# A two-layer recurrence on one core: x*Wx0 as 7 block products for 8, the second layer's recurrence in 256-column matmuls, the residual sums on GpSimd

## The chip, the cores and the metric

One of the eight NeuronCores of a Trainium2 chip runs the whole kernel. The time is the device time of one execution in microseconds (us). The kernel before took 2287.63 us (median of 3 runs, 2287.14 to 2290.14). The profiled execution took 2287.48 us; from its first to its last instruction, the span, it took 2285.6 us. TensorE's granted clock was 0.998 of full speed, its level of 2.4 GHz.

## The reference

`x` is 16 sequences of 512 steps of 512 values in float32. An LSTM of width 512 runs over it, its output is added to `x`, a tanh RNN of width 512 runs over the sum, and its output is added again.

```
# layer 0, for each step t
a = x[:, t] @ Wx0 + b0 + h @ Wh0                 # 16 x 2048
i, f, o = sigmoid(a[:, :1536]) in thirds;  g = tanh(a[:, 1536:])
c = f * c + i * g;   h = o * tanh(c);   y0[:, t] = x[:, t] + h
# layer 1, for each step s
k = tanh(k @ Wh1 + y0[:, s] @ Wx1 + b1);   y[:, s] = y0[:, s] + k
```

Both `h` and `k` start as `cond_1024`. No step of a layer can start before the state of the step ahead of it is there.

## The kernel before, in words

There are only 16 sequences, so TensorE gets the states as its stationary side (128 rows of the hidden dimension by 32 columns) and the weights stream past them. Four such matmuls run side by side, one for each 32 columns of the array (`tiles`, L175 to L180): they hold the same states, and each streams its own quarter (`q`) of the weights' columns into its own 32 partitions of a PSUM bank. "A group" below is such a set of four; a group with 256 columns covers 1024 outputs of one 128-row slice `k` of the contraction.

- **Input products, layer 0** (`input0`): two steps of `x` fill the 32 stationary columns. Four slices of 512 columns in float32 are the products of a pair of steps; one half of them is issued at every step. Each float32 matmul is issued as two instructions.
- **Recurrence, layer 0** (`recurrent0`): the state is split into a high and a low float16 part (2 x 16 columns), and so are the weights (`wh0_part`). A step has 2 halves of the outputs x 4 slices x 2 weight parts = 16 groups of 256 columns. The first half of the outputs holds all gates of the first half of the hidden units. ScalarE first writes the input products and the bias into the bank (`seed0`), the matmuls add to it.
- **Layer 1** runs `LAG` = 4 steps behind: `input1`, 2 groups of 128 columns in float32 a step, and `recurrent1`, 4 slices x 2 weight parts of 128 columns in float16.

TensorE's order in a step t is `recurrent0(t)`, a half of `input0` for a later pair, a half of `input1`, `recurrent1(t-4)`. While it does the last three, the cell of step t is worked out, one half of the hidden units after the other: VectorE turns the bank (`turn0`) and adds high and low part (`add0`); ScalarE does the gates (`gates`); VectorE the cell (`gate_products`, `cell`); ScalarE `tanh_cell`; VectorE the new state, rounded (`state_high`) and in full, and its low part (`state_low`), which sets `h0_ready[half]`. `recurrent0(t+1)` waits for `h0_ready[0]` ahead of slice 0 and for `h0_ready[1]` ahead of slice 2. Each engine follows its own written order (the `for t` loops at the end of each block), held to the others by semaphores alone.

The names in the profile are those of the tiles: `rec_ps` the banks of layer 0's recurrence, `in_ps` its input products, `rnn_ps` the bank that layer 1 uses for everything, `turned` what `turn0` (L353) or `turn1` (L403) wrote, `pre_sb` and `gate_ps` what `add0` (L359) wrote, `pre` what `add1` (L407) wrote, `uv` and `gates_cell` gates and cell. L365 is `gate_products`, L370 `cell`, L381 and L382 `state_high`, L389 `state_low`, L397 `add_y0`, L425 `add_y1`. All matmuls of the loop have the line L178.

## Time and profile before

| | |
|---|---|
| median of 3 runs | 2287.63 us |
| profiled execution, its span | 2287.48 us, 2285.6 us |
| TensorE matmul busy | 2242.9 us, 98% |
| VectorE busy | 1974.7 us, 86% |
| ScalarE busy | 1642.1 us, 72% |
| GpSimd busy | 1.8 us |
| TensorE's clock | 0.998 |

A busy share says how long an engine had something in it. Whether it sets the time is told by the chain of waits: who waited, for whom, and how long. "Idle before" in a group's row is the time that its engine stood still just ahead of it. Starts in a timeline are us from the start of the span.

### The profile page before, as it was taken

To read this page: it belongs to the slowest core of one execution; us is meant where nothing else is said; L and a number is where in the kernel's file an instruction comes from. 1 tells how busy PE (TensorE), PEld (TensorE's weight loads), DVE (VectorE), ACT (ScalarE), POOL (GpSimd) and SP (SyncE) were. 2 spreads that over 40 slices of the span, in tenths; PEclk is the share of its full clock that TensorE was granted. 3 is DMA by queue.
4 is the path that set the end of the run, shared out by engine and by line. 5 is a ranking of instruction groups with operands and counts; after the bars stand their busy time and mean duration, and the time that the engine had idled before them with its cause. 6 is when DMAs were issued, how large, how long until landed. Compare 5 with 4: busy or idle time off the path is not lost.

```text
span 2285.6 us, 150617 instructions
## 1 busy us (share of the span) xinstructions
PE 2242.9 (98%) x65564; PEld 1617.4 (71%) x65564; DVE 1974.7 (86%) x10283; ACT 1642.1 (72%) x5662; POOL 1.8 (0%) x10
## 2 busy tenths in 40 slices
PE   5999999999999999999999999999999999999997
PEld 2677777777777777777777777777777777777775
DVE  6888888888888888888888888888888888888887
ACT  5777777777777777777777777777777777777775
POOL 0000000000000000000000000000000000000000
PEclk9999999999999999999999999999999999999999
DMA  5000000000000000000000000000000000000000
GB/s 209 9 23 18 23 18 23 13 18 23 23 18 20 16 18 23 22 19 13 18 23 23 18 23 13 18 23 23 18 13 18 23 23 18 23 14 18 23 13 13
DMA packets 16738, 54.03 MB, mean 24 GB/s; under 512 B 2256, under 2 KB 2384, under 8 KB 14800
## 3 DMA queue, kind: packets, MB, share of 16 engines
q1 hardware_dynamic: 16080, 44.41, 5.5%
q8 instruction: 517, 8.47, 1.5%
q14 instruction: 141, 1.16, 0.2%
HBM read 27.62 MB, written 16.78 MB: 19 GB/s over the span
## 4 chain that ended last, share of the span: by engine, by line
PE 97%; DVE 2%; ACT 1%; issue 1%; POOL 0%; DVEq 0%; ACTq 0%; POOLq 0%
PE rec_ps L178 39%; PE in_ps L178 38%; PE rnn_ps L178 20%; ACT wh_part L478 1%; DVE largest_slice L277 0%; DVE turned L353 0%; DVE wh_part L321 0%; DVE uv L365 0%; DVE h_parts L381 0%; DVE pre_sb L359 0%; ACT gates_cell L502 0%; DVE h_parts L389 0%; ACT wx_sb L466 0%; DVE turned L403 0%; ACT rnn_ps L498 0%
## 5 line engine op out<-in xcount | busy, mean ns | idle before, releaser
L178 PE MATMUL in_ps<-wx_sb,x_sb 128*32 128x512 f32 x8192 | 977.4, 594 | 22.4 <-ACT wx_sb L466 22.4
L178 PE MATMUL rec_ps<-wh_part,h_parts 128*32 128x256 f16 x32704 | 988.9, 273 | 4.4 <-DVE h_parts L389 4.4
L178 PEld LDWEIGHTS rec_ps<-wh_part,h_parts 128*32 128x32 f16 x32704 | 867.5, 97 | 12.1 <-issue 7.0
L353 DVE STREAM_TRANSPOSE turned<-rec_ps 128x256 f32<-128x256 f32 x1024 | 460.4, 450 | 201.2 <-PE rec_ps L178 155.7
L178 PEld LDWEIGHTS in_ps<-wx_sb,x_sb 128*32 128x32 f32 x8192 | 258.9, 110 | 332.1 <-issue 318.9
L178 PEld LDWEIGHTS rnn_ps<-wx_sb,y 128*32 128x32 f32 x8192 | 247.0, 110 | 302.6 <-issue 301.1
L488 ACT ACTIVATE rec_ps<-in_ps,mask_scaled 128x256 f32<-128x256 f32 x1022 | 405.8, 434 | 2.0 <-PE in_ps L178 1.6
L178 PE MATMUL rnn_ps<-wh_part,h_parts 128*32 128x128 f16 x16352 | 323.4, 219 | 7.9 <-DVE h_parts L417 7.9
L178 PE MATMUL rnn_ps<-wx_sb,y 128*32 128x128 f32 x8192 | 318.4, 273 | 1.3 <-ACT rnn_ps L498 1.3
L502 ACT ACTIVATE gates_cell<-gate_ps,unscale 128x128 f32<-128x128 f32 x511 | 187.5, 367 | 181.2 <-DVE gate_ps L359 181.2
L498 ACT ACTIVATE rnn_ps<-rnn_ps,mask_scaled 128x128 f32<-128x128 f32 x511 | 174.8, 342 | 188.4 <-DVE turned L403 188.1
L178 PEld LDWEIGHTS rnn_ps<-wh_part,h_parts 128*32 128x32 f16 x16352 | 287.6, 97 | 9.2 <-ACT rnn_ps L498 5.5
L502 ACT ACTIVATE gates_cell<-pre_sb,unscale 128x128 f32<-128x128 f32 x511 | 205.3, 402 | 120.6 <-DVE pre_sb L359 120.5
L507 ACT ACTIVATE o_scaled<-gates_cell 128x32 f32<-128x32 f32 x1024 | 226.5, 221 | 16.1
L365 DVE SCALAR_TENSOR_TENSOR uv<-gates_cell 128x64 f32<-128x64 f32 x1024 | 227.2, 222 | 1.8 <-ACT gates_cell L502 1.3
L370 DVE SCALAR_TENSOR_TENSOR gates_cell<-uv 128x32 f32<-128x32 f32 x1024 | 196.8, 192 | 35.1
L389 DVE TENSOR_TENSOR h_parts<-h_full,h_parts 128x32 f16<-128x32 f32 x1024 | 192.0, 187 | 18.9
L512 ACT ACTIVATE tanh_c_sb<-gates_cell 128x32 f32<-128x32 f32 x512 | 117.6, 230 | 106.8 <-DVE gates_cell L370 106.7
L549 ACT ACTIVATE h_full<-pre,unscale 128x64 f32<-128x64 f32 x511 | 172.2, 337 | 2.3 <-DVE pre L407 2.3
L403 DVE STREAM_TRANSPOSE turned<-rnn_ps 128x128 f32<-128x128 f32 x512 | 162.0, 316 | 12.4 <-PE rnn_ps L178 3.2
L359 DVE TENSOR_TENSOR gate_ps<-turned 128x128 f32<-128x128 f32 x512 | 153.5, 300 | 17.6
L469 ACT ACTIVATE in_ps<-b_sb 128x512 f32<-128x512 f32 x256 | 150.9, 590 | 0.1
(52 smaller groups left out, 1272.9 us busy)
## 6 DMA issues: line engine op xcount, KB each, us to landing
x_sb<-xT SPq DMA_DIRECT2D x32, 512.0 KB, 3.7
yT<-y SPq DMA_DIRECT2D x64, 256.0 KB, 2.0
wh_sb<-wh SPq DMA_DIRECT2D x5, 1024.0 KB, 9.6
wx_sb<-wx SPq DMA_DIRECT2D x5, 1024.0 KB, 18.1
b_sb<-b SPq DMA_DIRECT2D x1, 256.0 KB, 2.7
b_sb<-b SPq DMA_DIRECT2D x1, 64.0 KB, 12.2
h_first<-h0T SPq DMA_DIRECT2D x1, 32.0 KB, 19.9
```

What stands on the lines that cost most here:

```text
L178: last = nc.tensor.matmul(out[QUAD * q:QUAD * (q + 1)], states, weights(q), start=False, stop=True, tile_position=(0, QUAD * q), skip_grou ...
L353: nc.vector.transpose(turned0[:, half].rearrange("p b n -> p (b n)"), rec0_ps[t % 2][half][:, 0:COLSH]).then_inc(turned0_done[half], 1)
L359: nc.vector.tensor_tensor(slices(pre0[half]), turned0[:, half, :, 0:BATCH], turned0[:, half, :, BATCH:], ALU.add).then_inc(pre0_done[half], 1)
L365: nc.vector.scalar_tensor_tensor(uv[:, half], gates_cell[:, half, 0:2], 1.0, gates_cell[:, half, 3:5], ALU.add, ALU.mult).then_inc(uv_done ...
L370: nc.vector.scalar_tensor_tensor(gates_cell[:, half, GATES], uv[:, half, 1], 0.5, uv[:, half, 0], ALU.mult, ALU.add).then_inc(cell_done[ha ...
L389: nc.vector.tensor_tensor(h0_parts[:, subs, BATCH:], slices(h0_full[:, cols]), h0_parts[:, subs, 0:BATCH], ALU.subtract).then_inc(h0_ready ...
L403: nc.vector.transpose(turned1[:, :].rearrange("p b n -> p (b n)"), rec1_ps).then_inc(turned1_done, 1)
L488: last = nc.scalar.activation(rec0_ps[t % 2][half][:, 0:COLSH], in0_ps[t // PAIR % 2][:, half * COLSH:(half + 1) * COLSH], ACT.Copy, scale ...
L498: nc.scalar.activation(rec1_ps, in1_ps[s // PAIR % 2], ACT.Copy, scale=own).then_inc(seed1_done, 1)
L502: nc.scalar.activation(gates_cell[:, half, 0:GATES].rearrange("p g n -> p (g n)"), pre0[half], ACT.Tanh, scale=unscale[0][:, :] if t else ...
L507: nc.scalar.activation(o_scaled[:, half], gates_cell[:, half, 2], ACT.Copy, bias=H_SCALE / 2, scale=H_SCALE / 2).then_inc(o_scaled_done[ha ...
L549: nc.scalar.activation(h1_full[:, :], pre1[:, :], ACT.Tanh, scale=unscale[1][:, :] if s > 1 else 1.0).then_inc(h1_full_done, 1)
```

## The change

**Seven products.** Four steps of `x` (a `SPAN`) are two pairs: the upper and the lower block row of a matrix X; the contraction has two halves, and so have the 512 columns. X*Wx0 is then a product of 2x2 blocks, done with 7 products and sums of blocks. Each is 2 slices of 256 columns: 14 units of one group, issued 4, 3, 4 and 3 to a step (`UNITS_OF_PART`), where the two pairs had 8 groups of 512 columns before. The sums of the blocks of `x` (`sum_x`, four for each 16 steps) and of the weights (`sum_wx0`, four at the start) are made by GpSimd. The sums on the side of the result are made where they accumulate (`z`, `v`, `c11`, `c12` in PSUM): ScalarE copies once or twice (`copy_v`, `begin_c11`), VectorE adds twice for each four steps (`begin_c12`, `finish_c22`). Two of the four `rec_ps` banks go to make room: the second half of layer 0 has one bank for all steps, and its seed is written in its own step.

**Layer 1.** High and low weights lie next to each other (`wh1_parts`): 4 groups of 256 columns for 8 of 128. Their sums are then four numbers for each output; one `tensor_reduce` adds them after a turn twice as wide. `seed1` writes half of the seed to each part.

**y.** `add_y0` and `add_y1` go to GpSimd, `add_y0` as two operations; VectorE's `h0_full` now waits for GpSimd to have read the one before (`h0_unscaled`). `input1` is split 3 slices and 1 for 2 and 2, so that each step has the same work. In `state_high` the full state becomes a step of its own, `state_full`, and the order of the second part of VectorE's step changes.

```diff
+SPAN = 2 * PAIR
+SPANS, PER_CHUNK = STEPS // SPAN, CHUNK // SPAN
+UNITS_OF_PART = (0, 4, 7, 11, 14)
+SLOTS = SPAN * SPANS - 5
...
+            def sum_wx0(i):
+
+                b11, b12 = wx0_sb[:, 0:SUBH, :, 0:COLSH], wx0_sb[:, 0:SUBH, :, COLSH:COLS]
+                b21, b22 = wx0_sb[:, SUBH:SUB, :, 0:COLSH], wx0_sb[:, SUBH:SUB, :, COLSH:COLS]
...
+                one, other = ((b12, b11), (b22, wx0_sums[:, 0]), (b22, b12), (b21, wx0_sums[:, 1]))[i]
+                nc.gpsimd.tensor_tensor(wx0_sums[:, i], one, other, ALU.subtract).then_inc(wx0_summed, 1)
...
+            for i in range(4):
+                sum_x(0, i)
+            reduce_largest(0)
+            for i in range(4):
+                sum_wx0(i)
...
+                nc.gpsimd.tensor_scalar(h0_true[:, :], h0_full[:, :], 1.0 / H_SCALE, None, ALU.mult).then_inc(h0_unscaled, 1)
+                pool.wait_ge(h0_unscaled, t + 1)
+                nc.gpsimd.tensor_tensor(y0[:, t // PAIR % Y0_PAIRS, :, t % PAIR], slices(h0_true[:, :]),
+                                        x_sb[:, v % 2, :, t % CHUNK], ALU.add).then_inc(y0_done, 1)
...
+            for t in range(END):
+                s = t - LAG
+                if 1 <= s:
+                    add_y1(s - 1)
+                if t < STEPS:
+                    add_y0(t)
+                if t == 1:
+                    reduce_largest(1)
+                v, c = divmod(t, CHUNK)
+                if 3 <= c < 7 and v + 1 < CHUNKS:
+                    sum_x(v + 1, c - 3)
...
+                products = (
+                    (z, lambda k: x_pair(g, 0, k), wx0_block(0, 0)),
+                    (v_ps[g % 2], lambda k: x_sum(g, 0, k), wx0_sum(0)),
+                    (z, lambda k: x_sum(g, 1, k), wx0_sum(1)),
+                    (c11_ps, lambda k: x_pair(g, 0, SUBH + k), wx0_block(1, 0)),
+                    (z, lambda k: x_sum(g, 2, k), wx0_sum(2)),
+                    (c12_ps, lambda k: x_sum(g, 3, k), wx0_block(1, 1)),
+                    (z, lambda k: x_pair(g, 1, SUBH + k), wx0_sum(3)),
+                )
...
-                        for part in weights:
-                            last = tiles(rec1_ps, states[:, k], lambda q: part[:, k, q])
+                    if s:
+                        last = tiles(rec1_ps, h1_parts[:, k], lambda q: wh1_parts[:, k, q].rearrange("p b w c -> p (b w c)"))
...
+                nc.vector.tensor_tensor(c12_ps, z_ps[g % 2], v_sb[:, :], ALU.add).then_inc(c12_begun, 1)
...
+                nc.vector.tensor_tensor(c22_sb[g % 2][:, :], z_ps[g % 2], v_sb[:, :], ALU.add).then_inc(c22_done, 1)
...
+            def state_full(half, n):
+
+                cols, subs = state_cols(half)
+                if n > 1:
+                    dve.wait_ge(h0_unscaled, n - 1)
                 nc.vector.tensor_tensor(h0_full[:, cols], o_scaled[:, half], tanh_c[half],
                                         ALU.mult).then_inc(h0_full_done[half], 1)
...
-                nc.vector.tensor_tensor(slices(pre1[:, :]), turned1[:, :, 0:BATCH], turned1[:, :, BATCH:],
-                                        ALU.add).then_inc(pre1_done, 1)
+                nc.vector.tensor_reduce(slices(pre1[:, :]), turned1[:, :, :, :].rearrange("p b r n -> p b n r"),
+                                        mybir.AxisListType.X, ALU.add).then_inc(pre1_done, 1)
...
+                    g, part = divmod(t + 5, SPAN)
+                    if t < SLOTS:
+                        if part == 2:
+                            begin_c12(g, t)
+                        elif part == 3:
+                            finish_c22(g, t)
                     turn0(0, t)
...
                     gate_products(1, n)
+                    state_high(0, n)
                     cell(1, n)
-                    state_high(0, n)
-                if rnn_state:
-                    add_y1(s - 1)
-                if lstm:
+                    state_full(0, n)
                     state_low(0, n)
                     state_high(1, n)
+                    state_full(1, n)
                     state_low(1, n)
                 if rnn:
                     turn1(s)
-                if lstm:
-                    add_y0(t)
-                if rnn:
                     add1(s)
...
+                if t < STEPS:
+                    act.wait_ge(slot_done, slots_until(t - 1))
...
+                    seed0(1, t)
+                    if ahead and part == 2:
+                        copy_v(g)
+                    if t + 1 < STEPS:
+                        seed0(0, t + 1)
```

Three places show how instructions move. The first is VectorE in the middle of the program, from the second half's gate products to the first turn of the next step. Before (L381 is `state_high` with the full state behind it in L382, L389 `state_low`, L425 and L397 the sums for y):

```order
L365 SCALAR_TENSOR_TENSOR uv<-gates_cell 128x64 [waits gates_done_1]
L370 SCALAR_TENSOR_TENSOR gates_cell<-uv 128x32 [waits uv_done_1]
L381 TENSOR_TENSOR h0_parts<-o_scaled,gate_ps 128x2x16 [waits tanh_c_done_0,o_scaled_done_0]
L382 TENSOR_TENSOR h0_full<-o_scaled,gate_ps 128x32
L425 TENSOR_TENSOR y1<-y0,h1_full 128x4x16
L389 TENSOR_TENSOR h0_parts<-h0_full,h0_parts 128x2x16 [waits h0_full_done_0]
L381 TENSOR_TENSOR h0_parts<-o_scaled,tanh_c_sb 128x2x16 [waits tanh_c_done_1,o_scaled_done_1]
L382 TENSOR_TENSOR h0_full<-o_scaled,tanh_c_sb 128x32
L389 TENSOR_TENSOR h0_parts<-h0_full,h0_parts 128x2x16 [waits h0_full_done_1]
L403 STREAM_TRANSPOSE turned1<-rnn_ps 128x128 [waits rec1_done]
L397 SCALAR_TENSOR_TENSOR y0<-h0_full,x_sb 128x4x16
L407 TENSOR_TENSOR pre1<-turned1 128x64 [waits turned1_done]
```

The same stretch of the changed program, where the next step is one with `begin_c12` (L519); L547 is `state_high`, L554 `state_full`, L561 `state_low`, L536 `cell`:

```order
L531 SCALAR_TENSOR_TENSOR uv<-gates_cell 128x64 [waits gates_done_1]
L547 TENSOR_TENSOR h0_parts<-o_scaled,gate_ps 128x2x16 [waits tanh_c_done_0,o_scaled_done_0]
L536 SCALAR_TENSOR_TENSOR gates_cell<-uv 128x32 [waits uv_done_1]
L554 TENSOR_TENSOR h0_full<-o_scaled,gate_ps 128x32 [waits h0_unscaled]
L561 TENSOR_TENSOR h0_parts<-h0_full,h0_parts 128x2x16 [waits h0_full_done_0]
L547 TENSOR_TENSOR h0_parts<-o_scaled,tanh_c_sb 128x2x16 [waits tanh_c_done_1,o_scaled_done_1]
L554 TENSOR_TENSOR h0_full<-o_scaled,tanh_c_sb 128x32 [waits h0_unscaled]
L561 TENSOR_TENSOR h0_parts<-h0_full,h0_parts 128x2x16 [waits h0_full_done_1]
L567 STREAM_TRANSPOSE turned1<-rnn_ps 128x256 [waits rec1_done]
L571 TENSOR_REDUCE pre1<-turned1 128x64 [waits turned1_done]
L519 TENSOR_TENSOR c1_ps<-in0_ps0,v_sb 128x256 [waits seed0_done_1,v_copied,slot_done]
L505 STREAM_TRANSPOSE turned0<-rec0_first_ps1 128x256 [waits rec0_done_0]
```

The first half's `state_high`, which waits for ScalarE's tanh, now stands ahead of the second half's `cell`; the two y sums are gone; two of four steps have a 256-column addition ahead of `turn0(0)`.

GpSimd at the start of the changed program (before, it had two ISA rows with the IOTA between them, and then the two reductions `largest_all`). An "ISA" row without names is a change of GpSimd's code library:

```order
L190 ISA
L190 IOTA partition 128x1
L223 TENSOR_TENSOR b0_diff<-b0_sb 128x256 [waits b0_doubled]
...
L209 TENSOR_TENSOR x_sums<-x_sb,x_sums 128x256 [waits x_summed]
L193 ISA
L193 ISA largest_all0<-largest0 128x1 [waits largest_done]
L220 ISA
L220 TENSOR_TENSOR wx0_sums<-wx0_sb 128x2048 [waits wx0_doubled]
...
L244 TENSOR_TENSOR y0<-h0_true,x_sb 128x4x16 [waits h0_unscaled]
L193 ISA
L193 ISA largest_all1<-largest1 128x1 [waits largest_done]
L242 ISA
```

There are now five changes of library for two, and three of them are behind the first sums.

## Rows read from the trace of the kernel before

**Rows 1.** The page: busy us, share of the span and instructions by engine.
```profile
PE 2242.9 (98%) x65564; PEld 1617.4 (71%) x65564; DVE 1974.7 (86%) x10283; ACT 1642.1 (72%) x5662; POOL 1.8 (0%) x10
```
**Rows 2.** Waits, whole span: us in total, times, longest.
```profile
PE rec_ps L178 <- DVE h_parts L389: 4.4, 6, 1.6
```
**Rows 3.** Timeline of TensorE, one step: start us, us, engine line op.
```profile
1201.05 1.93 PE L178 MATMUL rec_ps<-wh_part,h_parts 128*32 128x256 f16 x64
1202.79 1.90 PE L178 MATMUL in_ps<-wx_sb,x_sb 128*32 128x512 f32 x16
1204.51 0.62 PE L178 MATMUL rnn_ps<-wx_sb,y 128*32 128x128 f32 x16
1204.94 0.63 PE L178 MATMUL rnn_ps<-wh_part,h_parts 128*32 128x128 f16 x32
1205.39 1.93 PE L178 MATMUL rec_ps<-wh_part,h_parts 128*32 128x256 f16 x64
```
**Rows 4.** Timeline of the last steps, where TensorE has no input0.
```profile
2260.76 0.45 DVE L353 STREAM_TRANSPOSE turned<-rec_ps 128x256 f32<-128x256 f32 x1
...
2263.03 1.93 PE L178 MATMUL rec_ps<-wh_part,h_parts 128*32 128x256 f16 x64 [0.31 <-DVE h_parts L389]
2263.15 0.19 DVE L389 TENSOR_TENSOR h_parts<-h_full,h_parts 128x32 f16<-128x32 f32 x1
2263.26 0.31 DVE L403 STREAM_TRANSPOSE turned<-rnn_ps 128x128 f32<-128x128 f32 x1
...
2265.01 0.45 DVE L353 STREAM_TRANSPOSE turned<-rec_ps 128x256 f32<-128x256 f32 x1
```
**Rows 5.** Timeline of ScalarE, the same step as Rows 3.
```profile
1204.20 0.20 ACT L512 ACTIVATE gate_ps<-gates_cell 128x32 f32<-128x32 f32 x1
...
1204.75 0.23 ACT L512 ACTIVATE tanh_c_sb<-gates_cell 128x32 f32<-128x32 f32 x1 [0.21 <-DVE gates_cell L370]
```
**Rows 6.** Timeline of VectorE, the same step and the start of the next.
```profile
1203.03 0.45 DVE L353 STREAM_TRANSPOSE turned<-rec_ps 128x256 f32<-128x256 f32 x1
...
1204.53 0.19 DVE L370 SCALAR_TENSOR_TENSOR gates_cell<-uv 128x32 f32<-128x32 f32 x1
1204.64 0.18 DVE L381 TENSOR_TENSOR h_parts<-o_scaled,gate_ps 128x32 f16<-128x32 f32 x1
1204.73 0.18 DVE L382 TENSOR_TENSOR h_full<-o_scaled,gate_ps 128x32 f32<-128x32 f32 x1
...
1205.09 0.19 DVE L381 TENSOR_TENSOR h_parts<-o_scaled,tanh_c_sb 128x32 f16<-128x32 f32 x1
...
1205.41 0.19 DVE L389 TENSOR_TENSOR h_parts<-h_full,h_parts 128x32 f16<-128x32 f32 x1
...
1206.50 0.45 DVE L353 STREAM_TRANSPOSE turned<-rec_ps 128x256 f32<-128x256 f32 x1 [0.30 <-PE rec_ps L178]
1206.98 0.30 DVE L359 TENSOR_TENSOR gate_ps<-turned 128x128 f32<-128x128 f32 x1
```
**Rows 7.** Groups by form: busy us, mean ns of one, idle before.
```profile
L277 DVE TENSOR_REDUCE largest_slice<-wh_sb 128x1 f32<-128x512 f32 x4 | 2.5, 676 | 0.0
L488 ACT ACTIVATE rec_ps<-in_ps,mask_scaled 128x256 f32<-128x256 f32 x1022 | 405.8, 434 | 2.0 <-PE in_ps L178 1.6 <-issue 0.2
L407 DVE TENSOR_TENSOR pre<-turned 128x64 f32<-128x64 f32 x512 | 115.5, 226 | 0.1
L321 DVE SCALAR_TENSOR_TENSOR wh_part<-wh_sb,w_scale,wh_part 128x512 f16<-128x512 f32 x20 | 13.7, 746 | 1.5 <-ACT wh_part L478 1.5
```
**Rows 8.** Timeline of the start, GpSimd and VectorE.
```profile
12.33 0.13 POOL L167 IOTA partition<- 128x1 int32 x1 [10.85 <-issue]
...
22.27 0.38 POOL L170 PARTITION_ALL_REDUCE largest_all<-largest  x1 [9.81 <-DVE largest L277]
49.80 0.35 POOL L170 PARTITION_ALL_REDUCE largest_all<-largest  x1 [27.15 <-DVE largest L277]
...
58.53 0.18 DVE L382 TENSOR_TENSOR h_full<-o_scaled,gate_ps 128x32 f32<-128x32 f32 x1
```

More of the change, by code:

```diff
@@ L167, in _, with reduce_largest @@
             nc.gpsimd.iota(partition[:, :], [[0, 1]], 0, 1).then_inc(numbered, 1)
[L168 removed]
+            def reduce_largest(l):
                 pool.wait_ge(largest_done, l + 1)
@@ L243, in _ @@
                     recurrent0(0, h_first, [wh0_sb])
-                    for half in range(HALVES):
-                        input0(1, half)
+                    pe.wait_ge(seed0_done[0], 2)
+                    pe.wait_ge(c11_begun, 1)
+                    units(1, 2, UNITS_OF_PART[2])
                 elif t < STEPS:
```

262 lines of the change are left out of this document (186 added, 76 removed).

## The prediction, made before the changed kernel was run

> **What bounds the kernel now.** I read the busy shares first [rows 1]: TensorE has work in 98% of the span. The waits say that this is a true bound: TensorE waits for VectorE's new state (L389) for 4.4 us in the whole span, 6 times [rows 2], all in the first and last steps. The timeline of a step then gives its four parts [rows 3]: recurrence 1201.05 to 1202.79 (1.74), input products to 1204.51 (1.72), layer 1's input products to 1204.94 (0.43), its recurrence to 1205.39 (0.45). A step is 4.34 to 4.35 us, and 512 of them are 2225 of the span's 2285.6.
>
> The question is what comes next when TensorE gets less work, and the end of the trace answers it. There TensorE has no input products, so the recurrence alone sets the pace, and from one turn of the second half to the next it takes 2265.01 - 2260.76 = 4.25 us, with TensorE idle for 0.31 just ahead of it, released by L389 [rows 4]. So the loop through the state (turn, add, gates, cell, tanh, state, 16 groups) leaves only 0.10 us a step. Whatever TensorE saves beyond that is lost, and whatever the change puts into the loop counts in full.
>
> **What TensorE saves.** A float32 group of 512 columns takes 1.72 / 2 = 0.86, so one of 256 is taken at 0.43; layer 1's groups of 128 take 0.43 / 2 = 0.215, the same for each column [rows 3], so nothing is lost by short pieces. Units are 14 in four steps, 3.5 x 0.43 = 1.505 for 1.72. Layer 1's recurrence is 4 groups at 1.74 / 16 = 0.109, 0.436 for 0.45. With 1.74 and 0.43 as before a step of TensorE is 4.11, and 4 + 1 units are as long as 3 + 3 (1.935), so it is the same in each step. That is 0.23 less, 118 us in 512 steps, if TensorE stayed the bound. It does not.
>
> **The loop through the state.** It goes from the second half's turn to L389 (1205.41 - 1203.03 = 2.39 [rows 6]), and from there to the matmuls of slice 2 and the next turn. Three parts of the change touch it.
>
> 1. *The order in VectorE's queue.* The product for the second half starts 1205.09, and its tanh ended 1204.75 + 0.23 = 1204.98 [rows 5, 6]: 0.10 from the tanh's end to the product. The first half's tanh ends 1204.20 + 0.20 = 1204.40 [rows 5], so the first half's product can't start before 1204.50. Before, `cell` of the second half stood ahead of it and began 1204.53. Now `cell` stands behind that product, at the 0.10 that separates two small operations (1204.64, 1204.73 [rows 6]): 1204.60. That is +0.07 in the loop, in every step. Bounds: 0 (the tanh is seen sooner when nothing stands ahead of it) and +0.18, the product's whole duration. Taking y1's sum out of this stretch brings nothing, since the second half's product waited for the tanh and not for VectorE.
> 2. *The slack left in the 4.25.* L389 ends 2263.34 and slice 2's matmuls follow at 2263.03 + 4 x 0.109 = 2263.47 [rows 4], in their turn and not late, so some of those 0.13 may be slack. Bounds: 0, all of it is needed; and 0.10, since VectorE follows what it waits for by 0.03 (1206.50 + 0.45 to 1206.98 [rows 6]). I take 0.035, nearer to the end that is TensorE's own row. An ordinary step of the loop is then 4.25 - 0.035 + 0.07 = 4.285, over TensorE's 4.11 already; its bounds are 4.15 (both gains) and 4.43 (the product's 0.18, no slack).
> 3. *VectorE itself, in the two of four steps with a 256-column sum ahead of `turn0`.* The queue from L389 on: +0.11 to layer 1's turn (2263.15 to 2263.26 [rows 4]); that turn, 0.45 as the other turns of 256 columns, +0.03; the `tensor_reduce` R less the 0.08 by which the next starts ahead of its end; the sum C less 0.08; `turn0` to `add0` 0.48 (1206.50 to 1206.98); `add0` 0.22 [rows 6]; from the second turn to L389 again 2.39 + 0.07. In sum 3.59 + R + C. R: 512 elements take 0.676 [rows 7]; an element costs (0.45 - 0.31) / 128 = 0.0011 in the turns of 256 and 128 [rows 4, 6], so 256 take 0.676 - 0.27 = 0.41; below, 0.23, the addition it takes the place of (L407); above, 0.68, as if the strided reads cost twice. C: `add0` has 128 elements and takes 0.30 [rows 6], 512 take 0.75 (L321), so 256 take 0.44; bounds these two. The step is 3.59 + 0.41 + 0.44 = 4.44. In the other two steps the same queue, without the sum, is 4.44 - (0.44 - 0.08) = 4.08, under 4.285, and costs nothing.
>
> The mean is (4.285 + 4.44) / 2 = 4.36, 0.015 over the 4.345 of before: in the 504 steps in full swing +7.5 us. By R's bounds: 4.26 and 4.285 give 4.285 (-30 us), 0.68 gives 4.35 and 4.71, mean 4.53 (+93). By C's: 4.30 (mean 4.29, -27) and 4.75 (+87).
>
> **What costs nothing.** ScalarE gets 4 copies of 256 columns in four steps, 0.43 each [rows 7], for two of 512, and a `seed1` of 256 columns for 128: at most 0.43 + 0.14 a step on 1642.1 / 512 = 3.2 [rows 1], 3.8 of 4.36, all of it between its second tanh and the next step's gates. With that cover gone it would hold up the gates by what is over. The second half's seed, now in its own step, is asked for 0.87 later than the first's. On GpSimd y is three small operations a step. No row shows one; the nearest are VectorE's of 32 elements (0.18) and the partition reduction (0.38 [rows 8]), so 0.2 to 0.4 each, 0.9 for all; y0 is due about 3 us after the state. Above 1.4 each the queue would not keep up.
>
> **The port.** From rows nothing can be said on VectorE beside a busy GpSimd, which was busy 1.8 us in all [rows 1]. The Trainium skill, page "SBUF — State Buffer", section "Who interferes with whom", says that a VectorE instruction with two SBUF inputs and a GpSimd instruction that reads SBUF exclude each other, the first holding the port to its end. This speaks against the change, whose loop is full of such instructions; no run here shows it yet. The mechanism, in this kernel and priced from rows, is rival 2.
>
> **The start.** GpSimd now has five changes of code library. The first lies in the 10.85 ahead of the IOTA, beside the weights' DMAs; the second was over by 22.27 and can't be seen [rows 8]. So one costs 0 to 10.85; I take 7. The second now starts behind the sums of x, which I put at 19 by their place behind four weight tiles in SyncE's queue, and the first reduction is then at 26 for 22.27: +3.5. The first span's products come in another order, +1.5 to `seed0(0)`. The second reduction was at 49.80; now it is at 49.8 + 5 + 7 = 61.8, and behind it stands one more change, then y0 of step 2, whose reading VectorE's full state of step 3 waits for: 61.8 + 0.4 + 7 = 69 for 58.53 [rows 8], +10.5 in all; with 0 it would be +2, with 10.85 for each some +21. The Trainium skill, page "GPSIMD Engine Reference", section "2.1 Instruction dispatch", puts the first call to a freshly loaded library at about 6 us; by it the start would be about +7, and no run here shows it yet. The weights' sums, 4 x 2048 elements, end before they are due or hold it up by 1 or 2 us, which these bounds take in. The end, five steps of layer 1 alone, gets 0.13 + 0.19 a step for the wider turn and the reduction: +1.5.
>
> **The sum.** 2285.6 + 7.5 + 10.5 + 1.5 = 2305 of span; 2287.5 less 2285.6 lies around it, so 2307 of time. The profiled execution is within 0.2 us of the median.
>
> **Rivals.**
> 1. *TensorE stays the bound* (the loop is shorter than I read it): 2287.5 - 118 + 12 = 2182. For it: the waits of before. Against it: the 4.25 at the end, measured with less load on VectorE than now.
> 2. *GpSimd delays VectorE.* The full state releases at once L389, which is in the loop, and GpSimd's scaling for y0; y1's sum comes when `add0` does. If an operation of 0.2 to 0.3 is ahead of either, VectorE waits for its rest. At 0.13 a step it is 504 x 0.13 = +65 over mine, 2372; in every second step, 2340. For it: the loop has no slack to hide it. Against it: L389 follows the full state by 0.03, which leaves GpSimd little to be ahead by.
> 3. *On the other side of before: the loop has no detour through the first half's product.* The place is `cell` of the second half. If VectorE sees the first tanh 0.03 after its end, as it sees its own results, and not 0.10, `cell` starts where it did and both kinds of step lose 0.07: mean 4.29, -28, time 2287.5 - 28 + 12 = 2272. It decides from 0.05 on, where it eats the +20. R or C at half the way to their lower bounds gives the same or more. A shorter library change adds 5 to 8 in its favour.
> 4. *The start is worse*, each change of library as long as the first: +21, 2318. It lies inside the forecast's own range.
>
> **Chances.** Mine (2288 to 2325) 0.45, GpSimd in the way (2325 to 2375) 0.2, R or C larger with the same outcome 0.07, rival 3 (2250 to 2283) 0.2, rival 1 0.08. A measurement here tells apart 0.2%, 4.6 us. Slower 0.67, the same 0.07 (the low end of mine and the top of rival 3), faster 0.26. The range that leaves 2 in 10 out: 2252 to 2365.
>
> **What will show it.** TensorE's `rec_ps` group should have an idle time of 0.15 to 0.35 a step, over 80 us in all, released by `state_low` (L561), where it had 4.4. Steps should be of two lengths, near 4.28 and 4.44, in pairs. In VectorE's timeline `cell` of the second half (L536) starts 0.10 behind L547, and L547 0.10 behind the tanh's end. TENSOR_REDUCE of L571 has a mean of 410 ns, L519 and L526 some 440. The y operations on GpSimd show 200 to 400 ns. The second reduction is late by 10 us or so at 60. I am wrong if TensorE's idle time stays small (rival 1), if the steps are near 4.29 (rival 3), or if L561 and `add0` show longer durations or gaps while GpSimd is busy (rival 2).

## The result and the profile after

| | before | after |
|---|---|---|
| time, median | 2288.89 us (2287.14 to 2290.31) | 2352.13 us (2351.15 to 2353.26) |
| profiled execution: span | 2285.6 us | 2350.2 us |
| second half's turn of step 8 | 80.1 us | 105.2 us |
| mean step from 8 to 500 | 4.353 us | 4.427 us |

The ratio is 1.0277, with a 95% interval of 1.0259 to 1.0295. The direction was forecast and the time lies in the range, but I forecast +19 us and it was +63. The turns of the second half divide the 64.6 us of span: 25.2 up to step 8, (4.427 - 4.353) x 492 = 36.7 in the loop, 2.7 behind step 500.

The changed kernel's page, busy time by engine and its first groups, which answer to [rows 1]:

```profile
PE 2250.4 (96%) x63548; PEld 1741.2 (74%) x63548; DVE 2194.5 (93%) x9514; ACT 1782.6 (76%) x5919; POOL 648.0 (28%) x1679
...
DVE 77%; PE 12%; issue 10%; DMA 0%; ACT 0%; POOL 0%; SPq 0%; POOLq 0%; DVEq 0%; ACTq 0%
...
L273 PE MATMUL rec_first_ps<-wh_part,h_parts 128*32 128x256 f16 x16352 | 562.9, 275 | 52.9 <-DVE h_parts L561 27.2
```

VectorE has 86% turned into 93%, and the chain that ended last runs through it for 77% of the time; before, TensorE had 97% of it. So the bound has changed engine. TensorE's busy share of 96% hides that, since the ends of its matmuls are modelled. Its wait stands at the weight loads, on average 0.31 us in each of 491 steps, where I forecast 0.15 to 0.35. No releaser is shown for it; of the idle time of the matmuls themselves, 52.9 us, the row above puts 27.2 down to `state_low` (L561). The rows of the waits, after and before, which answer to [rows 2]:

```profile
PEld rec_first_ps L273 <- issue: 153.8, 491, 12.5
```
```profile
PEld rec_ps L178 <- issue: 11.6, 18, 3.0
```

The place of that wait differs from the one in the forecast. From step 100 to 480 the first matmul of `recurrent0`, which waits for the first half's state, starts 0.28 behind the one ahead of it (a matmul that waits for nothing follows by about 0.09); the first one of slice 2, which waits for the second half's state, starts 0.13 behind.

Two steps in four are long, as forecast. VectorE's timeline over one of them, which answers to [rows 6]:

```profile
1204.53 0.19 DVE L547 TENSOR_TENSOR h_parts<-o_scaled,gate_ps 128x32 f16<-128x32 f32 x1
1204.63 0.19 DVE L536 SCALAR_TENSOR_TENSOR gates_cell<-uv 128x32 f32<-128x32 f32 x1
...
1205.62 0.44 DVE L567 STREAM_TRANSPOSE turned<-rnn_ps 128x256 f32<-128x256 f32 x1
1206.10 0.59 DVE L571 TENSOR_REDUCE pre<-turned 128x64 f32<-128x256 f32 x1
1206.62 0.42 DVE L519 TENSOR_TENSOR c_ps<-in_ps,v_sb 128x256 f32<-128x256 f32 x1
1206.95 0.43 DVE L505 STREAM_TRANSPOSE turned<-rec_first_ps 128x256 f32<-128x256 f32 x1
1207.41 0.30 DVE L511 TENSOR_TENSOR gate_ps<-turned 128x128 f32<-128x128 f32 x1
```

From L567 to L511 VectorE never stands still for more than 0.04: its own queue is what lasts. `cell` (L536) stands 0.10 behind L547, as forecast. The groups by form, which answer to [rows 7]:

```profile
L571 DVE TENSOR_REDUCE pre<-turned 128x64 f32<-128x256 f32 x512 | 305.9, 597 | 17.4
L519 DVE TENSOR_TENSOR c_ps<-in_ps,v_sb 128x256 f32<-128x256 f32 x127 | 53.6, 422 | 0.0
L472 DVE SCALAR_TENSOR_TENSOR wh_part<-wh_sb,w_scale,wh_part 128x512 f16<-128x512 f32 x16 | 27.9, 1811 | 1.3 <-ACT wh_part L648 1.3
```

R is 597 ns where I put 410. L472, the low parts of `wh0` in the start, had a mean of 746 before [rows 7], here of 1811. The mean hides two sizes, as the view of that line shows (ns: least, median, most):

```profile
L472 DVE SCALAR_TENSOR_TENSOR wh_part<-wh_sb,w_scale,wh_part x16: 740/746/5042, 30.2 to 57.8; 128x512 f16<-128x512 f32 x16
```

Twelve of the 16 take 740 to 751; the other four take 4977 to 5042, one beside each of GpSimd's four sums of weights. The start on GpSimd and VectorE, which answers to [rows 8], first GpSimd, then VectorE:

```profile
28.10 0.38 POOL L193 PARTITION_ALL_REDUCE largest_all<-largest  x1 [10.25 <-issue]
35.96 4.56 POOL L220 TENSOR_TENSOR wx_sums<-wx_sb 128x2048 f32<-128x2048 f32 x1 [7.49 <-ACT wx_sb L624]
...
50.52 4.82 POOL L220 TENSOR_TENSOR wx_sums<-wx_sb,wx_sums 128x2048 f32<-128x2048 f32 x1
...
74.61 0.38 POOL L193 PARTITION_ALL_REDUCE largest_all<-largest  x1 [6.16 <-issue]
82.11 0.41 POOL L242 TENSOR_SCALAR h_true<-h_full 128x64 f32<-128x64 f32 x1 [7.13 <-issue]
```
```profile
33.11 2.74 DVE L472 SCALAR_TENSOR_TENSOR wh_part<-wh_sb,w_scale,wh_part 128x512 f16<-128x512 f32 x4 [0.15 <-ACT wh_part L648]
36.09 22.46 DVE L472 SCALAR_TENSOR_TENSOR wh_part<-wh_sb,w_scale,wh_part 128x512 f16<-128x512 f32 x8 [0.23 <-ACT wh_part L648]
```

Three library changes show (10.25, 6.16 and 7.13). And four low parts took 2.74 up to the moment at which GpSimd's sums of weights begin (35.96); the next eight took 22.46, to 58.55, of which the first four take 5.0 each, and the last four, behind the end of those sums at 55.34, 0.74 each.

### The profile page after: what moved, and what is told of

It is laid out like the page before. It is cut to its first block, busy times and chain, and to the rows that moved or that the text cites. A ratio compares the mean times of both kernels' runs of the same rounds, so it can differ in the third digit from the quotient of the medians.

```text
span 2350.2 us, 149629 instructions
## 1 busy us (share of the span) xinstructions
PE 2250.4 (96%) x63548; PEld 1741.2 (74%) x63548; DVE 2194.5 (93%) x9514; ACT 1782.6 (76%) x5919; POOL 648.0 (28%) x1679
## 4 chain that ended last, share of the span: by engine, by line
DVE 77%; PE 12%; issue 10%; DMA 0%; ACT 0%; POOL 0%; SPq 0%; POOLq 0%; DVEq 0%; ACTq 0%
DVE turned L505 14%; DVE h_parts L547 7%; DVE h_parts L561 7%; DVE turned L567 7%; DVE pre L571 6%; DVE uv L531 6%; DVE gate_ps L511 6%; DVE gates_cell L536 6%; DVE pre_sb L511 5%; DVE h_full L554 4%; PE rec_first_ps L273 3%; PE in_ps L273 3%; DVE h_parts L581 3%; PE rec_second_ps L273 3%; PE rnn_ps L273 2%
## 5 line engine op out<-in xcount | busy, mean ns | idle before, releaser
L273 PE MATMUL rec_first_ps<-wh_part,h_parts 128*32 128x256 f16 x16352 | 562.9, 275 | 52.9 <-DVE h_parts L561 27.2
L273 PE MATMUL rec_second_ps<-wh_part,h_parts 128*32 128x256 f16 x16352 | 537.7, 273 | 0.0
L273 PEld LDWEIGHTS rec_first_ps<-wh_part,h_parts 128*32 128x32 f16 x16352 | 362.0, 95 | 229.2 <-issue 152.4
L273 PEld LDWEIGHTS rec_second_ps<-wh_part,h_parts 128*32 128x32 f16 x16352 | 439.9, 97 | 9.0
L273 PE MATMUL in_ps<-wx_sums,x_sums 128*32 128x256 f32 x6096 | 400.7, 380 | 0.0
L273 PE MATMUL rnn_ps<-wh_parts,h_parts 128*32 128x256 f16 x8176 | 323.8, 273 | 10.4 <-DVE h_parts L581 10.4
L571 DVE TENSOR_REDUCE pre<-turned 128x64 f32<-128x256 f32 x512 | 305.9, 597 | 17.4
L670 ACT ACTIVATE rnn_ps<-rnn_ps,mask_scaled 128x256 f32<-128x256 f32 x511 | 228.2, 447 | 32.4 <-DVE turned L567 14.2
L273 PEld LDWEIGHTS rnn_ps<-wh_parts,h_parts 128*32 128x32 f16 x8176 | 230.7, 97 | 14.7 <-issue 7.3
L567 DVE STREAM_TRANSPOSE turned<-rnn_ps 128x256 f32<-128x256 f32 x512 | 226.7, 443 | 4.0 <-PE rnn_ps L273 4.0
L561 DVE TENSOR_TENSOR h_parts<-h_full,h_parts 128x32 f16<-128x32 f32 x1024 | 196.7, 192 | 36.0
L505 DVE STREAM_TRANSPOSE turned<-rec_second_ps 128x256 f32<-128x256 f32 x512 | 228.5, 446 | 0.3
```

What stands on the lines that cost most here:

```text
L273: last = nc.tensor.matmul(out[QUAD * q:QUAD * (q + 1)], states, weights(q), start=False, stop=True, tile_position=(0, QUAD * q), skip_grou ...
L505: nc.vector.transpose(turned0[:, half].rearrange("p b n -> p (b n)"), rec0_ps(t, half)).then_inc(turned0_done[half], 1)
L561: nc.vector.tensor_tensor(h0_parts[:, subs, BATCH:], slices(h0_full[:, cols]), h0_parts[:, subs, 0:BATCH], ALU.subtract).then_inc(h0_ready ...
L567: nc.vector.transpose(turned1[:, :].rearrange("p b r n -> p (b r n)"), rec1_ps).then_inc(turned1_done, 1)
L571: nc.vector.tensor_reduce(slices(pre1[:, :]), turned1[:, :, :, :].rearrange("p b r n -> p b n r"), mybir.AxisListType.X, ALU.add).then_inc ...
L670: nc.scalar.activation(rec1_by_part, in1_by_part(s // PAIR % 2), ACT.Copy, scale=own).then_inc(seed1_done, 1)
```

## Experiments

All of them in one table. Turn 8 is the second half's turn of step 8; the mean step is from 8 to 500; "long" and "ordinary" are the means of the two steps of four with a 256-column sum and of the other two. Times are medians, and the ratio is to the kernel before in the same comparison.

| kernel | turn 8 | mean step | long, ordinary | us | ratio, 95% |
|---|---|---|---|---|---|
| after | 105.2 | 4.427 | 4.58, 4.27 | 2352.1 | 1.0277 (1.0259 to 1.0295) |
| order_back | 104.4 | 4.387 | 4.51, 4.26 | 2332.4 | 1.0190 (1.0175 to 1.0205) |
| layer1_back | 104.1 | 4.333 | 4.35, 4.32 | 2302.6 | 1.0056 (1.0038 to 1.0074) |
| both_back | 103.5 | 4.324 | 4.34, 4.31 | 2297.7 | 1.0048 (1.0029 to 1.0066) |
| layer1_alone | 80.3 | 4.344 | | 2287.4 | 0.9992 (0.9983 to 1.0001) |
| order_alone | 81.5 | 4.356 | | 2291.8 | 1.0013 (1.0003 to 1.0022) |
| y_pool_alone | 83.4 | 4.360 | | 2294.0 | 1.0024 (1.0014 to 1.0034) |
| y_back | 99.6 | 4.474 | 4.68, 4.27 | 2371.4 | 1.0363 (1.0348 to 1.0379) |
| seven_alone | 99.5 | 4.375 | 4.44, 4.31 | 2319.6 | 1.0136 (1.0121 to 1.0151) |
| wx_sums_vector | 96.3 | 4.423 | 4.58, 4.26 | 2342.2 | 1.0237 (1.0222 to 1.0252) |
| quarter_sum | 103.7 | 4.321 | 4.37, 4.27 | 2298.2 | 1.0046 (1.0031 to 1.0061) |
| two_adds | 106.0 | 4.617 | 4.77, 4.46 | 2448.0 | 1.0701 (1.0683 to 1.0719) |
| after_start | 83.0 | 4.421 | 4.58, 4.26 | 2328.2 | 1.0174 (1.0158 to 1.0189) |
| before_split | 81.3 | 4.395 | | 2313.9 | 1.0111 (1.0096 to 1.0126) |
| best | 83.0 | 4.329 | 4.36, 4.30 | 2282.3 | 0.9972 (0.9955 to 0.9989) |
| best_no_x | 82.8 | 4.315 | 4.32, 4.31 | 2274.2 | 0.9937 (0.9916 to 0.9958) |

**order_back**: the order of VectorE's queue, in the changed kernel.

```diff
                     gate_products(1, n)
-                    state_high(0, n)
                     cell(1, n)
+                    state_high(0, n)
```

> The changed kernel with one thing undone: the second half's cell again ahead of the first half's state_high in VectorE's queue. Queue theory (every step is the longest of TensorE's 4.11 us, the loop through the state, and VectorE's own queue; both of the last two pass through that cell): both kinds of step get 0.07 shorter, the mean 4.355 for 4.427, 2352 - 36 = 2316 us. Port theory (GpSimd's y operations hold VectorE up, and that is what was missing in the forecast): the order matters less, since what is lost is lost elsewhere; 2330 to 2352 us.

The long steps lost 0.07, as expected, the ordinary ones 0.01: 20 us in all, 16 less than I expected. The time lies in the range of the rival, but the steps do not bear the rival out: what was to come back in a long step came back in full. Why an ordinary one lost so little, TensorE's waits show: the order mostly moves them. Behind an ordinary step the first matmul of `recurrent0` starts 0.21 behind the one ahead of it, for 0.18 in the changed kernel, and the first of slice 2 0.09, for 0.13; the two together are 0.01 less. The slack of 0.035 that I took out of [rows 4] does not show either: with the old order an ordinary step is 4.26 (median 4.24), beside the 4.25 of those rows.

**layer1_back and both_back**: the second layer's recurrence as before, in the changed kernel, and with the old order.

```diff
-                        last = tiles(rec1_ps, h1_parts[:, k], lambda q: wh1_parts[:, k, q].rearrange("p b w c -> p (b w c)"))
...
+                    for part in (wh1_part if s else [wh1_sb]):
+                        last = tiles(rec1_ps, (h1_parts if s else h_first)[:, k], lambda q: part[:, k, q])
...
-                nc.vector.tensor_reduce(slices(pre1[:, :]), turned1[:, :, :, :]..., ALU.add)
+                nc.vector.tensor_tensor(slices(pre1[:, :]), turned1[:, :, 0:BATCH], turned1[:, :, BATCH:], ALU.add)
```

> The changed kernel with layer 1's recurrence as before: 8 groups of 128 columns, a turn of 128 columns (0.32 us for 0.44) and one tensor_tensor (0.23) for the tensor_reduce (0.60). y stays on GpSimd. Queue theory: VectorE's queue in the steps with a 256-column sum falls from 4.58 to 4.08, under the loop's 4.27, so all steps become 4.27: 2352 - 79 - 2 = 2271 us. Port theory: the reduction was long because GpSimd reads beside it, what it held up stays held up, and the steps with a sum stay over 4.4: 2310 us or more.

> Both undone, the order and layer 1; the seven products and y on GpSimd stay. Queue theory: all steps 4.20, 2352 - 115 - 2 = 2235 us, under the kernel before. Port theory: 2270 us or more. If TensorE were the bound it would be 4.12 a step, 2195 us.

The second layer's part costs 49.5 us in the changed kernel, 46 of them in the loop, more than the whole loss of 36.7 there. But the two missed by 32 and 63, and neither rival is borne out: the steps with a sum are at 4.35, not over 4.4. The 5 us between the two kernels are not clear of the noise (2293 to 2311 and 2297 to 2305). Without VectorE as the bound the median step is 4.25 to 4.26 (I had put 4.20 for both_back), and single ones last up to 5.8 in layer1_back and 5.5 in both_back.

**layer1_alone, order_alone, y_pool_alone**: one part each, put into the kernel before, where TensorE is the bound.

> The kernel before with only layer 1's part: 256-column matmuls, the turn of 256 columns, one tensor_reduce; GpSimd does nothing in the loop. Theory that the reduction is slow by itself (four elements for each of 64 results, strided): its mean is 580 ns here too, VectorE's queue just fits into the step and the time is 2288 to 2296 us. Theory that GpSimd beside it makes it slow: its mean is near 410 ns, and the time is 2288 us.

> The kernel before with only VectorE's order changed as in the changed kernel: the first half's state_high ahead of the second half's cell. The cell starts 0.07 us later. Slack theory (the loop has 0.10 us a step under TensorE's step): hidden, 2288 us, within 3. No slack: 0.07 x 512 = +36, 2324 us.

> The kernel before with only the sums for y on GpSimd. Queue theory: the steps stay at 4.35 us and only the start is longer, by the two changes of GpSimd's library around the second reduction, some 6 us: 2295 us. Port theory: VectorE's operations with two inputs beside GpSimd's get longer or late; 0.05 us a step or more beyond the slack is 2315 us or more.

All three within 0.3% of the kernel before, and near what I expected (order_alone is 3.8 over 2288, where I had said within 3): each part alone is hidden behind TensorE or costs a few us of start. In layer1_alone GpSimd does nothing in the loop, and the reduction still takes 591 ns: it is slow by itself. With y on GpSimd (y_pool_alone) the step of the loop is 4.360 for 4.353, although VectorE's addition L438 stands beside GpSimd's for y in almost every step:

```profile
1206.79 0.23 DVE L438 TENSOR_TENSOR pre<-turned 128x64 f32<-128x64 f32 x1
1206.79 0.40 POOL L189 TENSOR_TENSOR y<-h_true,x_sb 128x64 f32<-128x64 f32 x1
```

In 489 of 492 steps VectorE's starts first; it keeps its 0.226, and GpSimd's takes 0.39 on average, for the 0.32 that it takes where nothing is in its way.

**y_back and seven_alone**: y's sums back on VectorE; and with that both_back, so only the seven products are left of the change.

> The changed kernel with the sums for y back on VectorE, where they stood before; GpSimd keeps only the sums for the seven products. Queue theory: y0's sum fits into the wait for the turn, y1's into the wait for the tanh, the steps stay at 4.42 to 4.43; the start is some 6 us shorter, since VectorE no longer waits for y0 behind the changes of library: 2345 us. Port theory: the steps fall to 4.36 or less, 2315 us or less.

> Only the seven products (with GpSimd's sums of x and of the weights); layer 1, the order and y as in the kernel before. Queue theory: no step is held by VectorE's queue, the loop with y1's sum in it is 4.25 as at the end of the trace of before, the start is some 20 us longer: 2288 - 50 + 20 = 2258 us. If TensorE were the bound: 2195 us. If the 256-column sums cost their full length in VectorE's queue (0.34 us in two of four steps): 2320 us.

y_back is 19 us slower than the changed kernel, where I expected 7 less. That is not what y's sums cost on VectorE: outside the steps with sums of x the steps are those of the changed kernel (the medians of the long and the ordinary ones are 4.57 and 4.25 in both). The 23 us that its loop is longer by lie in two steps of sixteen, which last 5.05 and 4.88, and in these stand GpSimd's sums of x; in the changed kernel the waits of y's operations on GpSimd keep the four of them a step apart.

seven_alone missed by 62. Its time is just that of the last rival, 2320, but by luck: its steps with a 256-column sum have the same median, 4.26, as the others. Its timeline has one reason for the miss:

```profile
275.31 0.73 POOL L208 TENSOR_TENSOR x_sums<-x_sb 128x256 f32<-128x256 f32 x1 [65.76 <-DMA x_sb<-xT]
275.43 0.66 DVE L499 SCALAR_TENSOR_TENSOR gates_cell<-uv 128x32 f32<-128x32 f32 x1
...
276.12 0.72 POOL L208 TENSOR_TENSOR x_sums<-x_sums,x_sb 128x256 f32<-128x256 f32 x1
...
276.21 0.72 DVE L558 TENSOR_TENSOR y<-y,h_full 128x64 f32<-128x64 f32 x1
276.80 0.72 POOL L208 TENSOR_TENSOR x_sums<-x_sb 128x256 f32<-128x256 f32 x1
276.85 0.72 DVE L522 TENSOR_TENSOR h_parts<-h_full,h_parts 128x32 f16<-128x32 f32 x1
```

GpSimd's sums begin first, and beside them `cell` (L499) and `state_low` (L522), operations of 0.19, take 0.66 and 0.72, and y's sum (L558), one of 0.22, takes 0.72: each ends 0.05 to 0.09 behind GpSimd's. With GpSimd otherwise empty the four sums follow each other as soon as x has arrived, and that step lasts 6.1 us. The 42 steps with such sums are 32 us longer in all than the median step; the other 25 us over the median are single long steps, of which more below.

**wx_sums_vector**: the collision in the start, with the sums of `Wx0` on VectorE.

```diff
-                nc.gpsimd.tensor_tensor(wx0_sums[:, i], one, other, ALU.subtract).then_inc(wx0_summed, 1)
+                nc.vector.tensor_tensor(wx0_sums[:, i], one, other, ALU.subtract).then_inc(wx0_summed, 1)
```

> The changed kernel with the four sums of blocks of Wx0 taken on VectorE, after the low parts of wh0, for GpSimd. Nothing else moves. Port theory (GpSimd's sums and VectorE's two-input operations exclude each other in the start): the 16 low parts, mean 1811 ns in the changed kernel and 746 in the kernel before, come back to about 750, which gives back 12 to 17 us; the four sums on VectorE take about 2.3 us each (the reductions of 2048 elements take 2.29), so 9 us of it are paid again: the second half's first turn comes at about 54.5 for 59.15, the time is about 2347.5. Rival (the low parts are slow by themselves, or wait for ScalarE's high parts): they stay near 1800 ns, and the time is 2352 + 9 = 2361.

```profile
L459 DVE SCALAR_TENSOR_TENSOR wh_part<-wh_sb,w_scale,wh_part 128x512 f16<-128x512 f32 x16 | 11.0, 748 | 1.5 <-ACT wh_part L649 1.3
```

From 1811 back to 748 ns, and 10 us less in the time, though VectorE has 9 us more to do. The mechanism holds; the gain is larger than the 4.6 us that I expected: the first turn comes at 51.2, not at 54.5.

**quarter_sum and two_adds**: the size of R. In the first, two of four slices are left out of the sum.

```diff
-                nc.vector.tensor_reduce(slices(pre1[:, :]), turned1[:, :, :, :]..., ALU.add)
+                nc.vector.tensor_tensor(slices(pre1[:, :]), turned1[:, :, 0], turned1[:, :, 2], ALU.add).then_inc(pre1_done, 1)
```

```diff
+                nc.vector.tensor_tensor(half_sums[:, :, :, :], turned1[:, :, 0:2], turned1[:, :, 2:4], ALU.add).then_inc(half_summed, 1)
+                dve.wait_ge(half_summed, s + 1)
+                nc.vector.tensor_tensor(slices(pre1[:, :]), half_sums[:, :, 0], half_sums[:, :, 1], ALU.add).then_inc(pre1_done, 1)
```

> The changed kernel with the sum over four slices of the second layer's turned result taken over two slices only, by the 64-element addition that the kernel before has (225 ns for 597); the other two slices are left out of the sum. Theory (the size of this one operation is what I got wrong in the loop): the two steps of four that last 4.59 and 4.57 fall by 0.37 until the way round through the state holds at 4.27, so all steps are about 4.27, and the loop gives back (4.427 - 4.27) x 492 = 77 us: 2275. Rival (the long steps come from something else, TensorE's order or the sum of the first layer's 256 columns): they stay above 4.45, and the time above 2320.

> The changed kernel with the sum over four slices taken by two additions in a row, 128 elements and then 64, with nothing left out. From VectorE's rows (an addition of 128 elements 0.29, of 64 elements 0.225, the wait between dependent operations 0.03, and the overlap of some 0.1 between operations in a row) the pair takes 0.48 to 0.53 from start to end for 0.597 + 0.03: 0.08 to 0.13 less in the long steps, half of that per step, 20 to 32 us: 2325. Rival (the cost of an operation is mostly per instruction): 0, 2352.

The groups of quarter_sum, then of two_adds:

```profile
L571 DVE TENSOR_TENSOR pre<-turned 128x64 f32<-128x64 f32 x512 | 189.3, 370 | 17.4
```
```profile
L572 DVE TENSOR_TENSOR half_sums<-turned 128x128 f32<-128x128 f32 x512 | 225.1, 440 | 17.4
L574 DVE TENSOR_TENSOR pre<-half_sums 128x64 f32<-128x64 f32 x512 | 165.5, 323 | 17.6
```

The addition of 64 elements takes 370 here and 226 in the kernel before [rows 7]. A step of two_adds shows why:

```profile
1466.51 0.32 POOL L245 TENSOR_TENSOR y<-h_true,x_sb 128x64 f32<-128x64 f32 x1
1466.53 0.45 DVE L572 TENSOR_TENSOR half_sums<-turned 128x128 f32<-128x128 f32 x1
1467.02 0.22 DVE L574 TENSOR_TENSOR pre<-half_sums 128x64 f32<-128x64 f32 x1
```

It starts just behind GpSimd's addition for y and takes 0.45; `add0`'s second addition, of the same 128 elements with GpSimd still, takes 0.29. Which of the two begins first decides: in 457 of 492 steps GpSimd's does, and L572 takes 0.45 and ends 0.15 behind it; in 29 VectorE's does, and it takes 0.29. L574 takes 0.225 with GpSimd still and 0.64 in the 118 steps in which a sum of x has begun ahead of it.

So two_adds missed its forecast by 123 us, the other way. From the start of the pair to the start of the next operation there are 0.63 us (median), where the `tensor_reduce` leaves 0.51: both kinds of step are longer by 0.11 in the median. The other 40 us or so of the loop's 93 lie in the steps with sums of x.

The same collision in quarter_sum (GpSimd first in 457 steps, 0.38; VectorE first in 29, 0.226): R is less by 0.597 - 0.370 = 0.23, and the long steps fell by 0.21, from 4.58 to 4.37, not to the 4.27 that I expected of an addition of 0.225; the loop lost 52 us. So R counts in the long steps nearly in full, as the forecast's sum has it. Both other forms meet the collision, which the `tensor_reduce` at the same place (597 beside GpSimd, 591 without) does not.

**best and after_start**: the start. Both partition reductions stand ahead of GpSimd's first addition, and VectorE does the sums of the start. In best this stands on both_back, in after_start on the changed kernel.

```diff
-            for i in range(4):
-                sum_x(0, i)
-            reduce_largest(0)
-            for i in range(4):
-                sum_wx0(i)
+            for l in range(2):
+                reduce_largest(l)
```

> The kernel with both parts undone (second layer as before, cell ahead of the first half's product, y on GpSimd, seven products; 2297.7 us, the eighth turn at 103.5) with another start: GpSimd has no additions ahead of its two partition reductions, which follow each other; the differences of the bias, the first chunk's sums of x and the sums of Wx0 are taken by VectorE, two of the latter after the first step. Theory of the start: the library changes between the reductions and the additions, and the collision of the two engines, are the 25 us that the start lost; now the eighth turn comes at 78 to 82, and the time is about 2275. If only half of it comes back: 2286. The loop stays as it was, 4.32 a step.

> The changed kernel with the start of best: both partition reductions ahead of GpSimd's first addition, the sums of the start on VectorE. Theory (library changes and the collision are all that the start lost): the eighth turn at 82 to 84 for 105.2, the loop at 4.43 a step as in the changed kernel, and 2352 - 22 = 2330. Rival (part of the loss is the seven products' own start, four accumulators in place of one): the eighth turn stays above 90, and 2337 or more.

Both starts come to turn 8 at 83.0; from the changed kernel 24 us come back, 22 were expected. So library changes and the collision together are all of the start's loss but 3 us. best missed its 2275 by 7, and its turn 8 the 78 to 82. It is the fastest kernel that computes everything, by 0.3% under the one before.

**before_split and best_no_x**: the single long steps of the kernels without VectorE as the bound.

```diff
-                    last = tiles(in0_ps[p % 2][:, 0:COLS], ..., lambda q: wx0_sb[:, k, q])
+                    for lo in (0, COLSH):
+                        last = tiles(in0_ps[p % 2][:, lo:lo + COLSH], ..., lambda q: wx0_sb[:, k, q, lo:lo + COLSH])
```

> The kernel before with each 512-column matmul of x*Wx0 cut into two of 256 columns: the same columns, 144 matmuls and weight loads each per step for 128, nothing else. Theory (TensorE's instructions come in packets of 16 KB, 256 instructions, and at more than about 65 instructions per us a packet comes too late now and then): the rate goes from 59 to 66 per us, single steps of 4.4 to 5 us appear in which a gap of TensorE ends 1.2 to 1.5 us after a packet has arrived; mean step 4.37 to 4.45 for 4.347 and 2300 to 2340. Rival (columns alone count): steps stay even at 4.35, and the time is 2288 to 2291.

> The kernel best (2282.3) with the loads of x from the third chunk on cut to one step of one slice: the sums and products then use old x, which is left out of the computation. Theory that the large loads (512 KB, every 16 steps) delay the packets of instructions: the longest steps (at 160, 176, 224, 336 and others that lie within 6 us of a load) go, the steps' mean falls from 4.33 to 4.28, and the time to 2258. If the packets are late by themselves: 4.33 and 2282, with the spread of 20 us between executions kept.

Cutting the matmuls in two, with not one column more, costs 26 us, as the theory had it and not the rival. The median step is 4.36, and 21 of 492 last 4.65 to 5.29. Their gaps on TensorE have no releaser. The longest in both_back, in TensorE's timeline:

```profile
762.57 0.84 PE L272 MATMUL rec_first_ps<-wh_part,h_parts 128*32 128x256 f16 x24
764.44 0.40 PE L272 MATMUL rec_first_ps<-wh_part,h_parts 128*32 128x256 f16 x8 [1.04 <-issue]
```

And both_back's DMA queues from 757.8 to 762.1, then from 762.1 to 763.1:

```profile
q1 hardware_dynamic: 135, 0.51, 36.9%
q14 instruction: 1, 0.01, 0.6%
```
```profile
q8 instruction: 1, 0.02, 5.8%
q1 hardware_dynamic: 7, 0.01, 4.0%
```

That the queue q8 brings TensorE's instructions I read from its count: it has 517 packets of 16 KB for the 131,128 matmuls and weight loads of the kernel before, and 581 for the 147,512 of before_split, 254 each in both. Usually one starts every 3.9 us in both_back. Here a load of x (0.51 MB) lies in the way, no packet starts for 5.4 us, and TensorE stands still in the middle of a group until 1.4 us after the packet has landed. Of the 20 longest steps between 8 and 500, all in both_back and all in before_split have their widest gap between starts of matmuls end 1.2 to 1.6 us behind such a packet, and none in order_back, which has 16 matmuls a step less than both_back. Of both_back's 366 steps under 4.3 us 43 do, which is what chance gives (0.4 of 3.9 us). This is a match in time, and before_split's longer time agrees with it; no run changes the packets alone. best_no_x missed its 2258 by 16: the loads of x are at most 8 us of it, by medians, with 29 of 34 steps over 4.65 left, and best's own executions spread over 20 us.

## Why the forecast had the sign and not the size

- *What bounds* was right. TensorE's saving of 118 us came to nothing, through the loop of 4.25 us that the end of the trace showed.
- *R* failed: this is the step of the prediction that makes most of the miss. The term 0.41 measured 0.597. I took the rate per element of a reduction that reads linearly to one result; this one makes 64 results, and reads four elements 64 bytes apart for each. Which of the two makes it long no run shows. The long step, forecast as 3.59 + R + C = 4.44, comes to 4.61 with R = 0.597 and C = 0.42, and was 4.58. The loop is 29 us of the 45 by which I was short, the start 15, the end 1. My own upper bound, "0.68, as if the strided reads cost twice", was nearer than my 0.41.
- *The path through the state* was right in the long steps only, where the order cost 0.07 (order_back), as worked out. In the ordinary ones it cost 0.01, and no slack shows. My path ran through the second half's state and slice 2 alone; TensorE's wait stands mostly ahead of slice 0, where the first half's state is due, and the new order only moves a part of it from there to slice 2. That the ordinary step, forecast 4.285, was 4.27 is luck: 0.07 too much less 0.035 that wasn't there.
- *C*, forecast 0.44 and measured 0.42, was right, and so was y on GpSimd, nearly: 0.37 + 0.32 + 0.36 = 1.05 us where I put 0.9, off the path.
- *The start* failed: forecast +10.5, measured +25.2. The library changes were sized about right (7 each, measured 6 to 10), but I let the sums of the weights cost "1 or 2 us". They took 4 x 4.8 us on GpSimd, and beside each of them one of VectorE's low parts took 5.0 for 0.75, so that the 16 of them took 27.9 us for 11.0. The first turn came 17.8 later than before, and with the sums on VectorE, 9 us of work, it is still 8.0 earlier (wx_sums_vector, 51.2 for 59.1), so nearly all of the 17.8 is the collision. The other 7.4 lie between the first turn and step 8, where the second reduction stands with its two library changes; y_back, in which VectorE waits for nothing behind them, gets 5 of these back (41.0 us from the first turn to turn 8, for 46.1; 38.7 before).
- *Rival 2*, GpSimd in VectorE's way, had the measured time in its interval and is not what happened in the loop: at the places that I named, L389's and `add0`'s, no operation is longer by more than 5 ns on average in the changed kernel (L561 192 for 187 ns, L511 292 to 301 for 292 to 300). What happened is the case of a larger R, to which I gave 0.07, with a longer start on top. The collision itself is real, in places that I did not name: the start, the sums of x, and an addition of VectorE ahead of which GpSimd's has begun. L561 stands beside GpSimd's scaling for y in 457 of 492 steps and starts first in all of them. The Trainium skill, page "SBUF — State Buffer", section "Who interferes with whom", says that two-input operations of VectorE and GpSimd's reading exclude each other; the rows of wx_sums_vector (1811 to 748) and two_adds (0.45 for 0.29) agree with it, and so does the reduction with its one input, which is untouched. One input alone is no safeguard, though: y_back's `tensor_scalar` of 64 elements (L551) takes 0.40 for 0.15 in the 22 steps in which it stands beside a sum of x.
- *Rival 3* took the loop's detour at 0.07 and forecast 2272 without it; order_back is 2332. The detour was no more than a third of the loss, 20 us of 63.

What stays open: why before_split's packets come late, since each takes 1.07 us (median) and its 254 instructions are 3.9 us of work; and what holds the ordinary step of both_back and best at 4.25, since none of their runs changes it. How far ahead the engine asks for them no run shows. Nor was a `tensor_reduce` to 64 results with linear reading tried, since the transposition sets the order; it would tell strided reading from the number of results.

## What to carry to other kernels

When the bound leaves an engine, the next one must be priced by operations of the same form (access pattern and number of results), not only of the same size; where none is in the trace, take the whole range between the bounds and not a rate per element. Do not judge GpSimd's part by whether its operations stand beside VectorE's with two inputs, but by which begins first: in quarter_sum and two_adds VectorE's addition, begun behind GpSimd's, ended 0.08 to 0.15 us past GpSimd's end, and those that began ahead of it took no longer than usual. Short and spread operations cost little, long or bunched ones much (the sums of weights, the four sums of x). And put GpSimd's reductions together, ahead of its arithmetic, since each change of library took 6 to 10 us here. Count instructions as well as columns on an engine with no idle time: before_split has 16 more matmuls a step and not one column more, and is 26 us slower; the seven products alone bring 12 more.

## Hardware behaviour that I had not expected

- A reduction with strided reading of 4 for each of 64 results takes 591 to 597 ns; linear, 512 to one result take 676 [rows 7].
- Of an addition of VectorE's and one of GpSimd's that overlap, the one that begins second waits. GpSimd first: VectorE's ends 0.08 (64 elements, quarter_sum) or 0.15 (128, two_adds) behind it. VectorE first: it takes its usual 0.226, and GpSimd's ends 0.18 behind it (y_pool_alone).
- An operation behind the start of GpSimd's addition: 128 elements 0.45 for 0.29, 64 elements 0.38 for 0.23 (0.64 behind a sum of x), a low part of 512 elements 5.0 for 0.75 behind a sum of 2048. The `tensor_reduce`, the turns and the sums into PSUM were not longer (L519 in the changed kernel: 421 ns in the 30 steps beside a sum of x, 422 with GpSimd still).
- TensorE at 144 matmuls and 144 loads in 4.35 us (66 instructions per us, before_split) stands still at times for up to 0.7 us with no releaser, 1.0 in both_back; at 59 per us, in the kernel before, no idle time over 0.01 us shows in the loop.
- The spread between executions is 1 to 5 us in the kernels with VectorE's queue as the bound of the long steps, and up to 20 us (best, 2271.7 to 2291.6) in those with the late packets.
